# Second edge stage: one 128 x 260 product per tile, diagonal blocks copied out of PSUM by ScalarE

## The reference

```python
alpha = leaky_relu(a_src[src] + a_dst[dst], 0.2)          # per edge and head, 4 heads
amax  = segment_max(alpha, dst)
ex    = exp(alpha - amax[dst])
denom = segment_sum(ex, dst)
out   = segment_sum(x_lin[src] * (ex / denom[dst]), dst)  # 64 columns per head
```

## Time and profile before

| | us |
|---|---|
| median of 3 timed runs | 3599.06 (3598.24 to 3601.83) |
| recorded execution, span from first to last instruction | 3846.8 |
| second edge stage, its loop, in the recorded execution | 2645 to 3501 |

### The profile page before, as it was taken

The page is one execution under the profiler, slowest core; times in us unless marked ns, Lnnn a source line. Parts: engine busy times, 40 slices in busy tenths (PEclk is TensorE's granted clock), DMA queues, the critical chain, the costliest instruction groups (busy, mean ns, idle before and its releaser), DMA issues. The chain is left out here.

```text
span 3846.8 us, 54793 instructions
## 1 busy us (share of the span) xinstructions
PE 1901.0 (49%) x12473; PEld 1322.9 (34%) x12474; DVE 1938.2 (50%) x5547; ACT 806.2 (21%) x2540; POOL 2138.9 (56%) x2169
## 2 busy tenths in 40 slices
PE   0784430055555554338881018744555545552397
PEld 0443320044444443325551006432333333331275
DVE  8677970066566566302220173475555555555622
ACT  0341100033333332012220002201222222221122
POOL 1777777666666663277777727606665666660000
PEclk9996665567677676569996558865666566555599
DMA  4110000153233236333331201105322322273100
GB/s 165 17 20 3 2 2 2 17 163 83 82 83 84 79 82 50 115 76 71 74 72 15 70 21 22 16 0 113 78 75 73 77 76 75 74 76 57 51 14 20
DMA packets 178231, 225.58 MB, mean 59 GB/s; under 512 B 86005, under 2 KB 137713, under 8 KB 178056
## 3 DMA queue, kind: packets, MB, share of 16 engines
q0 software_dynamic: 83328, 140.71, 18.9%
q1 hardware_dynamic: 94852, 84.30, 7.7%
HBM read 185.01 MB, written 38.87 MB: 58 GB/s over the span
## 5 line engine op out<-in xcount | busy, mean ns | idle before, releaser
L234 POOL DMA_INDIRECT mid_sorted<-p_stage_rec,p_stage_row x528 | 656.2, 1243 | 201.6 <-issue 143.1
L2084 POOL DMA_INDIRECT e_rows<-mid_table,e_index x488 | 525.2, 1076 | 184.0 <-issue 137.1
L861 POOL DMA_INDIRECT e_rows<-mid_table,e_index x448 | 435.0, 971 | 166.4 <-issue 124.5
L2350 PE MATMUL e_ps_A<-e_rows,e_weight 128*32 128x65 f32 x3904 | 272.0, 293 | 354.7 <-issue 343.4
L234 POOL DMA_INDIRECT mid_sorted<-x_stage_rec,x_stage_row x272 | 323.3, 1189 | 102.3 <-issue 72.5
L1030 PE MATMUL e_ps_A<-e_rows,e_hot 128*125 128x260 f32 x896 | 369.1, 552 | 0.0
L2350 PEld LDWEIGHTS e_ps_A<-e_rows,e_weight 128*32 128x32 f32 x3904 | 166.5, 149 | 459.1 <-issue 459.1
L1015 PE MATMUL e_ps_T<-e_identb,e_hot 128*125 128x128 bf16 x454 | 95.9, 308 | 297.7 <-DVE e_hot L892 235.3
L2304 ACT ACTIVATE e_acc<-e_state 128x66 f32 x488 | 126.0, 258 | 525.1 <-issue 412.8
L1030 PEld LDWEIGHTS e_ps_A<-e_rows,e_hot 128*125 128x125 f32 x896 | 224.1, 277 | 33.9
L2117 DVE TENSOR_REDUCE e_found<-e_ps_S 128x64 f32<-128x192 f32 x61 | 21.8, 358 | 331.7 <-PE e_ps_S L2358 304.6
(11 more groups left out here) (517 smaller groups left out, 4464.6 us busy)
## 6 DMA issues: line engine op xcount, KB each, us to landing
e_rows<-mid_table,e_index POOLq DMA_INDIRECT x936
mid_sorted<-p_stage_rec,p_stage_row POOLq DMA_INDIRECT x528
mid_expert_in<-p_zrow SPq DMA_DIRECT2D x1, 8192.0 KB
w<-in_L_ffn_w SPq DMA_DIRECT2D x16, 512.0 KB
x_w<-in_L_ffn_w SPq DMA_DIRECT2D x16, 512.0 KB
x_xs<-mid_expert_in SPq DMA_DIRECT2D x64, 128.0 KB
x_b<-in_L_ffn_b SPq DMA_DIRECT2D x64, 128.0 KB
mid_expert_out<-x_y SPq DMA_DIRECT2D x64, 128.0 KB
```

Of the source, the lines that this page charges most:

```text
L234: pool.indirect_dma_start(out=to, out_offset=bass.IndirectOffsetOnAxis(ap=stage_row[:, half, j:j + 1].bitcast(U32), axis=0), in_=stage_rec ...
L861: pool.indirect_dma_start(out=rows[:, tile, :], out_offset=None, in_=k["table"], in_offset=bass.IndirectOffsetOnAxis(ap=index[:, half, j:j ...
L2084: pool.indirect_dma_start(out=rows[:, j, q, :], out_offset=None, in_=k["table1"], in_offset=bass.IndirectOffsetOnAxis(ap=index[:, j, q:q + ...
L2350: last = mm(sums_of(j)[h * B1:(h + 1) * B1, q // HALF, at:at + W1], weight[:, q, h * B1:(h + 1) * B1], rows[:, j, q, h * W1:(h + 1) * W1], ...
```

## The change

The sums of a tile become one product of all 128 weight columns with all 260 row columns. Of its 4 x 4 blocks only the four on the diagonal (head h's weights with head h's columns) are wanted. A tile fills a PSUM bank of its own, so four tiles, a half, are made at a time; ScalarE copies the four diagonal blocks of a half (32 partitions by 4 tiles by 65 columns each) into a new SBUF tile `taken`, and VectorE adds from there. TensorE makes the second half after `spread_to_edges`. `s_agg` counts halves instead of turns, a new semaphore `s_take` counts halves taken, and `keep_sums` is split in two halves of four.

```diff
+        taken = m.sb("taken", [P, 2, TG, W1])
...
-                    wait_alone(pool, s_agg, i - RING + 1)
+                    wait_alone(pool, s_agg, 2 * (i - RING + 1))
...
-                wait_alone(dve, s_agg, i + 1)
+                wait_alone(dve, s_take, 2 * i + 2)
...
-                v.scalar_tensor_tensor(state[:, j, q, 0:W1], before, scale[:, j, q:q + 1], sums_of(j)[:, q // HALF, q % HALF * W1:(q % HALF + 1) * W1],
+                v.scalar_tensor_tensor(state[:, j, q, 0:W1], before, scale[:, j, q:q + 1], taken[:, j % 2, q, :],
...
+            def take_heads(i, j, half):
+
+                if not (known(i) and i < 2):
+                    wait_alone(act, s_acc, (i - 1) * TG)
+                wait_alone(act, s_agg, 2 * i + half + 1)
+                for h in range(H):
+                    at = slice(h * B1, (h + 1) * B1)
+                    last = nc.scalar.activation(taken[at, j % 2, half * HALF:(half + 1) * HALF, :],
+                                                ps_A2[at, :, h * W1:(h + 1) * W1], ACT.Copy)
+                last.then_inc(s_take, 1)
+
+            def keep_sums(i, j, half):
+
+                wait_alone(act, s_acc, i * TG + half * HALF + HALF)
+                for q in range(half * HALF, (half + 1) * HALF):
...
+                adding = not (known(i) and (i < 1 or i > TURNS))
                 if not (known(i) and i < 3):
-                    keep_sums(i - 3, (j - 3) % RING)
+                    keep_sums(i - 3, (j - 3) % RING, 0)
                 if u is not None:
                     keep_hot(i + 1, (j + 1) % RING)
+                if adding:
+                    take_heads(i - 1, (j - 1) % RING, 0)
+                if u is not None:
                     act.wait_ge(s_spr, i + 1)
                     nc.scalar.activation(scale[:, j, :], drop[:], ACT.Exp).then_inc(s_scale, 1)
+                if adding:
+                    take_heads(i - 1, (j - 1) % RING, 1)
+                if not (known(i) and i < 3):
+                    keep_sums(i - 3, (j - 3) % RING, 1)
...
-            def add_up(i, j):
+            def add_up(i, j, half):
                 wait_alone(pe, s_wt, i + 1)
-                for q in range(TG):
-                    at = q % HALF * W1
-                    for h in range(H):
-                        last = mm(sums_of(j)[h * B1:(h + 1) * B1, q // HALF, at:at + W1], weight[:, q, h * B1:(h + 1) * B1],
-                                  rows[:, j, q, h * W1:(h + 1) * W1], start=True, stop=True)
+                if not (known(i) and i == 0 and half == 0):
+                    wait_alone(pe, s_take, 2 * i + half)
+                for q in range(half * HALF, (half + 1) * HALF):
+                    last = mm(ps_A2[:, q % HALF, 0:H * W1], weight[:, q, :], rows[:, j, q, 0:H * W1], start=True, stop=True)
                 last.then_inc(s_agg, 1)
...
-                    add_up(i - 1, (j - 1) % RING)
+                    add_up(i - 1, (j - 1) % RING, 0)
                 if u is not None:
                     spread_to_edges(i, j)
+                if not (known(i) and i < 1):
+                    add_up(i - 1, (j - 1) % RING, 1)
```

More of the change, by code:

```diff
@@ L2022, in stage_edges1 @@
         s_agg = m.sem("added_up")
+        s_take = m.sem("own_heads_taken")
         s_acc = m.sem("accumulated")
@@ L2048, in known @@
             return isinstance(i, int)
-        def sums_of(j):
-            return ps_A2[:, j % 2 * 2:j % 2 * 2 + 2]
         def tiles_of(t2, i, shift=0):
@@ L2295, in keep_hot @@
                 nc.scalar.activation(hotT[:, j], ps_hT[:], ACT.Copy).then_inc(s_hTk, 1)
-            def keep_sums(i, j):
-                wait_alone(act, s_acc, i * TG + TG)
-                for q in range(TG):
+            def take_heads(i, j, half):
[10 more added lines that the diff above has]
+                for q in range(half * HALF, (half + 1) * HALF):
                     block_of = act.value_load(k["bin1"][0:1, bass.ds(i * TG + q, 1)], min_val=0, max_val=G1_BINS - 1)
```

## The result

The changed kernel takes 3713.82 us (3711.76 to 3716.49, 4 runs) against 3600.44 (3598.24 to 3602.0, 4 runs): ratio 1.0317, 95% interval 1.0303 to 1.0332. It is 113 us slower; 134 were forecast.

What follows compares the result with a forecast made beforehand. GpSimd's gathers were taken to bound the kernel before at 11.5 us per turn; a loop through ScalarE's order makes it 13.7, 2.2 us x 61 turns = +134, so 3599 + 134 = 3733 us, range 3600 to 3840.

Steps and rivals of the forecast that it cites:

- Taking the 248 us off: Recorded span minus timed median, 247.7 us, taken as recording cost: 101 us in the first edge stage, 147 in the second.
- The first rival: Second edge stage: TensorE's gaps are real, timed turns are 14.3 us and the change removes them; 3562 or 3471 us; 14%.
- What bounds before: Second edge stage: GpSimd's gathers, not TensorE, set a timed turn of 11.0 to 11.9 us, taken as 11.5.
- The floor of 11.0: GpSimd per turn: 0.98 us from cast to first gather plus eight gathers with pauses, 10.0 us.
- The product: TensorE: the full product takes 0.82 us per tile, 3.3 us per half of four tiles, against 0.28 per tile before.
- The rule of four times the small product: TensorE, from the Trainium skill: full product 1.1 us per tile, 4.5 per half, turn about 15.8 us; not followed.
- The takes: ScalarE's eight new copies per turn, four per half: 1.2 us per half, 2.4 us per turn.
- The additions from SBUF: VectorE's eight additions: 0 to 50 ns off each, 0.4 us per turn at most; nothing taken.
- The loop: Closed once per turn through ScalarE's order: exponential, spreads, spreading product, second product half, take, four keeps, next exponential; 13.7 us.
- The branch: Before the second product half: spreading product ends at 6.6 us, first half is taken at 6.2 and doesn't delay it.
- The sum: Second edge stage: 13.7 - 11.5 = 2.2 us per turn x 61 = +134 us, giving 3733 us.

Runs made afterwards that it cites:

- the calm record: The kernel before run again with no edit, as a second profile of it: 3599.34 us, span 3597.6 us.
- the product alone: Kernel before with only the full product per tile, in before's order, no halves or takes, sums not the reference's: 3598.3 us against 3599.3, ratio 1.0001.
- opening the first alone: Kernel after with the next exponential ahead of take half 1 and the weighing waiting for the second product half: 3711.37 us, ratio 1.0313.

## Why the prediction was right, and where it wasn't

- **Taking the 248 us off.** The decision to forecast from the timed times and not from the recorded turn of 14.3 us was right for this comparison; the reason given, that recording makes the gaps, doesn't hold: on two chips timed runs take 3826 us, and the traces from there show the gaps. They are real in some executions. How the 248 us were shared out was nearly right: between the two records of before, 105 us lie ahead of the stage's first exponential (101 taken) and 142 in its 60 turns (147 taken). The timed runs of 3599 us were calm ones, and it is luck that those of the comparison were too: on the gapped chip the same change costs 272 us, twice the 134. The first rival said that real gaps make the change faster; it was wrong in its second half: on a gapped chip the change is slower by 7.1%.
- **What bounds before.** Right for calm chips: GpSimd's gathers, median turn 11.57 (11.5 taken; the mean is 11.82), shown by the index made ahead in before (-68 us) and by the product alone (nothing). The floor of 11.0 has one gap too many: turns of the first edge stage have a median of 10.7.
- **The product.** 0.82 us per tile was taken and 0.76 measured; 3.3 for a half, and 3.41 for the first and 2.71 for the second measured on average. The rule of four times the small product would have given 1.1, by 35 ns a record. In the calm record the small form takes 94.8 us for 3528 records, 0.21 us a tile, and 0.76 is 3.6 times that; in the turn shown it is 64 x 24 ns / 8 = 0.19, and the ratio 4.0. The Trainium skill's rule (TensorEngine Tiling (Array Packing), Theoretical Speedup: up to four times) is close to what the calm rows show; what failed in my use of it was the small form's price, read from a gapped record.
- **The takes.** Mis-sized: 1.55 us per half, not 1.2; the overlap of 0.10 us isn't there (4 x 378 ns are 1.51).
- **The additions from SBUF.** 283 ns against 278: no gain. The Trainium skill (Perfetto Trace Analysis, Optimizing Scalar/DVE Operations) gives VectorE about 125 ns of overhead on PSUM and 60 on SBUF, 65 less; these rows don't show it, and the measurement decides.
- **The loop.** Right that ScalarE's order closes it, and nearly right in its sum: 13.7 forecast, 13.82 in the turn shown, 13.58 on average. The keeps at its end are 2.15, not 2.5. The branch was wrong in most turns: the prediction had the first half taken at 6.2, ahead of the spreading product at 6.6, and the other order only for the lower clock. Measured, the second half starts 0.39 us behind the spreading product on average, because the take is 1.55 and the weights need 0.35 us to reach TensorE. That the shorter second half (2.71 for 3.3) makes up for it is luck. What the prediction missed is the second ring, about 1 us shorter in after, and as long as the first once that is opened, so that opening the first alone gives nothing.
- **The sum.** 1.76 us per turn instead of 2.2: the mean of before is 11.82 and not 11.5, since some single turns take over 12 us and seven of the last eight over 13, and after's is 13.58, not 13.7. That is 105.7 us in the turns, and 7.8 in the drain, which the prediction put at nothing.

## What to carry to other kernels

Before an in-order engine is given a copy that waits for a late product, list what stands behind it on that engine and follow it once around; a ring through the order costs its whole length every turn, while the same work outside it cost 14 us in all here instead of 113. Then look for branches and for a second ring of nearly the same length (here through shared PSUM banks) before moving anything, and read from the engine's idle time which of them binds. And when a profile's span and the timed runs differ, run the kernel again for a second record before reading "issue" gaps as a bound or as an artefact.

## What was not expected of the hardware

- Of the four chips that the record names, two ran the kernel before in 3826 us instead of 3600. Profiles there show gaps of about 0.7 us between TensorE's product records and on ScalarE's register operations, on VectorE's and SyncE's as well. In the first record of before 217 of the 254 of ScalarE's register operations that take over 0.4 us fall beside a gather of GpSimd (gathers fill 0.61 of the second edge stage's loop there); in the second record of before there is none over 0.4 us. Their cause is open.
- The same change is 3.2% slower on calm chips and 7.1% on a gapped one.
- With more work TensorE was granted more clock in the same stretch (0.62 to 0.79) and took 0.57 us for a product that took 0.76 in after, where the clock was 0.63 within the product's records and 0.83 here.
